# Cross attention of a decoder block: value rows (ctx times Wv Wo) first, then P times them, on one core

## The chip, the cores and the metric

One Trainium2 chip, one of its cores. The metric is device time in microseconds of one execution. Engines are named PE (TensorE, matrix products), ACT (ScalarE), DVE (VectorE), POOL (GpSimd) and SP (SyncE, which issues DMAs).

## What is computed

A decoder block on x (16 batches x 64 tokens x 256), all in float32: a chunked test-time-training attention, then cross attention to ctx (16 x 64 x 128) with 16 heads of width 128, then a gated FFN of 704 with quantised weights and activations. Each of the three is followed by adding its input and a layer norm. The change touches the cross attention alone:

```
q = rmsnorm(x @ Wq); k = rmsnorm(ctx @ Wk); v = ctx @ Wv      # 16 heads of 128
P = softmax(q k^T / sqrt(128))                                # 64 x 64 for each batch and head
out = concat_h(P_h v_h) @ Wo                                  # 2048 -> 256
```

For each head, `v_h` and its 128 rows of Wo come to `ctx (Wv_h Wo_h)`. Both kernels form `mvo`, the product Wv_h Wo_h (128 x 256 for each head, 4096 columns in all), once before the tiles.

## The kernel before

The first half (until about 179 us) is the test-time-training attention over 4 chunks, with key projections for the cross attention placed between its steps. It works in 32x32 blocks (L554, L562, L572): four blocks lie at the partitions 32j..32j+31, for the operands and the output alike, and write one PSUM bank.

The second half is a software pipeline over 8 tiles of 128 tokens (2 batches). `pipeline()` counts i from -2 to 10. In cycle i, PE works in an order that is written out by hand at L738 to L781: the q projection of tile i (`q_quarter`, four quarters of 512 columns, each two products, L626), the transposes of q (L640), the scores of tile i (`scores`, 64 columns for each head and batch, L658), the cross attention's rest for tile i-1, the FFN's gate and up for tile i-2 (`gate_up`, L699) and its down projection for tile i-3 (L717). The output projection of the first half (`ttt_out`, L723) and the transposes of the new x1 (L731) serve tiles i+2 and i+1. ACT and DVE have written-out orders of their own.

The rest of the cross attention for a tile is:

- softmax: DVE (L1379 to L1382, L1393), POOL (L1525, L1527) and ACT (L1011) make P of the scores, and signal `p_ready`;
- `p_transpose` (L649): 8 transposes of 128x128; ACT copies them out as `pt`;
- `context_sum` (L672): 4 products of 64 rows x 512 columns, P times ctx. n=0 and n=1 take the row halves 0..63 and 64..127 of `pt` and `ctx2` one after the other, n=2 and n=3 are placed apart. ACT copies each out as `cxp` (L1006);
- `attention_out` (L680): for each of 16 heads, one product 128x128 by 256 columns, `cxp` times `mvo`, all summed in one bank; eight heads before `x1_transpose` and eight behind it. DVE adds it to x1 (L1402).

PSUM banks: 0 and 1 hold q quarters, 2 and 3 the transposes, 4 and 5 the scores. Banks 6 and 7 are handed out in turns from a list, `turns`; a turn waits on PE until the turn two before it has been copied out (`open_turn`, L608). The list of before holds `down`, four `cp`, `wo`, four `gu` and `y` for each cycle.

The clock column (PEclk, 1.00 or 0.50) is the share of TensorE's 2.4 GHz that was granted. A float32 product of before stands in the trace as two records.

Of the kernel before, what the change touches and what calls it, by code (L numbers as in the profile page):

```python
# [58 lines left out]
def decoder_block(nc, x, ctx_in, Wq, Wk, Wv, Wo, Wbeta, ln_w, ln_b, Wg1, Wg2, norm_w,  # L59
                  XWq, XWk, XWv, XWo, gq, gk, w1_in, w2_in, out):  # L60
    stack = ExitStack()
    with stack:
# [65 lines left out]
        krow1 = place("krow1", BANK, over="ctxt")  # L128
# [63 lines left out]
        qjunk = place("qjunk", BANK)  # L192
        assert cursor[0] <= at_of["xwk"]
        cxp = place("cxp", XH * P)
        gs = place("gs", FF)
        assert cursor[0] <= at_of["pR"]
# [8 lines left out]
        sg = place("sg", FF)  # L205
# [86 lines left out]
        for i, cur, prev, last2, last3, nxt, nxt2 in pipeline():  # L292
            turns += [("down", i - 3, 0, "dve")] * last3
            turns += [("cp", i - 1, n, "act") for n in range(2)] * prev
            turns += [("wo", i + 2, 0, "dve")] * nxt2
            turns += [("cp", i - 1, n, "act") for n in range(2, 4)] * prev
            turns += [("gu", i - 2, n, "dve") for n in range(4)] * last2
            turns += [("y", i - 1, 0, "dve")] * prev
# [23 lines left out]
        def _(sp):  # L322
# [71 lines left out]
            for half in range(2):  # L394
                load(ctx2[half * T:(half + 1) * T, :].rearrange("p (b c) -> p b c", c=CD), ctx_in.rearrange("b s c -> s b c"), "ctx")
# [15 lines left out]
        def _(pe):  # L411
# [251 lines left out]
            def context_sum(i, n):  # L663
                b2, odd = n // 2, n % 2
                if n == 0:
                    pe.wait_ge(sem("tp_evac"), tp_of[("pt", i, 1)] + 1)
                    if i == 0:
                        pe.wait_ge(sem("ld_ctx"), 64)
                bk = open_turn("cp", i, n)
                rows = slice(odd * T, odd * T + T)  # L670
                b = 2 * i + b2
# [886 lines left out]
```

## Time and profile before

| | |
|---|---|
| median of 3 runs | 442.09 us (441.3 to 442.74) |
| the profiled execution | 441.95 us, span of its trace 440.1 us |
| busy: PE, DVE, ACT, POOL | 362.4, 266.0, 218.0, 120.9 us |
| mean granted TensorE clock | 0.919 |
| pipeline over the tiles | from about 179 us to the end |

PE's busy time is a union of overlapping records; how long a group really occupies PE is read from the start of the next group. A timeline row gives the start in the span, its length, the instructions, and in brackets the idle time of the engine before it with what ended it.

### The profile page before, as it was taken

How to read it: one execution, taken by the hardware profiler on the slowest of the kernel's cores; microseconds unless marked ns; L12 is line 12 of the kernel's file. 1: busy time of each engine (PE TensorE's matmuls, PEld its weight loads, DVE VectorE, ACT ScalarE, POOL GpSimd, SP SyncE). 2: the span in 40 equal slices, each digit the busy share in tenths (PEclk: the TensorE clock that was granted, in tenths of full speed). 3: DMA queues.
4: the chain of work that ended last, by engine and by line, in shares of the span. 5: the costliest groups of instructions: out<-in, count | busy, mean ns of one | idle time of the engine just before them, and what ended most of it. 6: DMA issues, size and time to landing. Idle time of an engine off the chain costs nothing.

```text
span 440.1 us, 10666 instructions
## 1 busy us (share of the span) xinstructions
PE 362.4 (82%) x4506; PEld 212.4 (48%) x4506; DVE 266.0 (60%) x494; ACT 218.0 (50%) x584; POOL 120.9 (27%) x132
## 2 busy tenths in 40 slices
PE   3999979779977735596799999999999999996942
PEld 2445844435433212343465665755757557473621
DVE  1579945499996886504243384673946728367564
ACT  3035954545533333063646757468475584753320
POOL 3042891022040041103033332343223432233001
PEclk9999969988968969589899999999999999998975
DMA  8990000000323001901010010100100100000000
GB/s 260 240 365 11 1 4 5 3 4 3 81 75 101 2 0 35 211 7 48 0 41 11 1 48 12 44 6 13 49 12 25 25 14 0 12 3 0 12 0 25
DMA packets 17630, 19.93 MB, mean 45 GB/s; under 512 B 3360, under 2 KB 15024, under 8 KB 17328
## 3 DMA queue, kind: packets, MB, share of 16 engines
q1 hardware_dynamic: 17552, 19.24, 16.0%
q8 instruction: 36, 0.59, 0.6%
q14 instruction: 10, 0.08, 0.1%
q10 hardware_dynamic: 32, 0.02, 0.0%
HBM read 18.07 MB, written 1.18 MB: 44 GB/s over the span
## 4 chain that ended last, share of the span: by engine, by line
PE 50%; DVE 19%; ACT 13%; POOL 8%; issue 7%; DMA 1%; SPq 1%; POOLq 0%; DVEq 0%; ACTq 0%
PE ps L626 9%; PE ps L535 7%; PE ps L672 5%; PE ps L446 5%; PE ps L525 4%; PE ps L680 3%; PE ps L640 3%; PE ps L572 3%; POOL pr L1525 3%; POOL pr L1527 3%; PE ps L554 3%; PE ps L649 2%; DVE pr L1382 2%; DVE pr L1379 2%; DVE mx L1381 2%
## 5 line engine op out<-in xcount | busy, mean ns | idle before, releaser
L626 PE MATMUL ps<-xwq,x1t 128*128 128x512 f32 x128 | 65.0, 638 | 0.9 <-ACT x1t L997 0.9
L680 PE MATMUL ps<-mvo,cxp 128*128 128x256 f32 x256 | 58.4, 382 | 0.1
L680 PEld LDWEIGHTS ps<-mvo,cxp 128*128 128x128 f32 x256 | 47.6, 190 | 6.7 <-issue 0.4
L535 PE MATMUL ps<-ctxt,xwk 128*128 128x512 f32 x64 | 39.0, 716 | 2.4 <-issue 2.2
L975 ACT ACTIVATE qjunk<-ps 128x128 f32<-128x128 f32 x128 | 33.5, 280 | 9.9 <-PE ps L626 9.7
L896 ACT ACTIVATE ksq<-ps 128x512 f32<-128x512 f32 x32 | 19.0, 594 | 38.3 <-PE ps L525 28.2
L626 PEld LDWEIGHTS ps<-xwq,x1t 128*128 128x128 f32 x128 | 24.0, 202 | 27.5 <-issue 24.7
L985 ACT ACTIVATE qt<-ps 128x512 f32<-128x512 f32 x32 | 19.2, 601 | 23.4 <-PE ps L640 23.3
L525 PE MATMUL ps<-ksq,onehot 128*32 128x512 f32 x64 | 21.8, 680 | 9.2 <-ACT ksq L896 9.1
L672 PE MATMUL ps<-pt,ctx 64*128 64x512 f32 x64 | 28.0, 657 | 0.2 <-ACT cxp L1006 0.2
L975 ACT ACTIVATION_READ_ACCUMULATOR qjunk<-ps 128x1 f32 x128 | 27.1, 212 | 0.0
L1525 POOL TENSOR_TENSOR pr<-pr,rq 128x1024 f32<-128x1024 f32 x7 | 13.3, 1901 | 49.1 <-DVE pr L1382 49.1
L1355 DVE TENSOR_TENSOR rr<-ps,xn 128x256 f32<-128x256 f32 x8 | 3.4, 424 | 34.6 <-PE ps L723 34.5
L1362 DVE TENSOR_TENSOR gs<-ps,s 128x352 f32<-128x352 f32 x16 | 8.4, 525 | 25.1 <-PE ps L699 25.1
L1519 POOL TENSOR_TENSOR rq<-rq,mhalf 128x16 f32<-128x16 f32 x8 | 23.3, 2909 | 0.7
L640 PEld LDWEIGHTS ps<-ident,qtok 128*128 128x128 f32 x128 | 15.3, 141 | 16.1 <-issue 12.8
L1508 POOL TENSOR_SCALAR rstd<-mv 128x1 f32<-128x1 f32 x24 | 5.3, 219 | 61.5 <-DVE mv L1318 61.5
L900 ACT ACTIVATE kt<-ps,gks 128x512 f32<-128x512 f32 x32 | 21.8, 682 | 0.0
L1006 ACT ACTIVATE cxp<-ps 128x512 f32<-128x512 f32 x32 | 18.9, 627 | 5.1 <-PE ps L672 5.1
L640 PE MATMUL ps<-ident,qtok 128*128 128x128 f32 x128 | 19.7, 277 | 0.9 <-ACT qtok L976 0.9
L997 ACT ACTIVATE x1t<-ps 128x256 f32<-128x256 f32 x8 | 3.1, 383 | 34.7 <-PE ps L731 34.7
L1323 DVE TENSOR_SCALAR x<-rr,mv,rstd 128x256 f32<-128x256 f32 x16 | 6.6, 413 | 22.5 <-POOL rstd L1509 22.5
(212 smaller groups left out, 736.5 us busy)
## 6 DMA issues: line engine op xcount, KB each, us to landing
rkb<-kscale SPq DMA_DIRECT2D x16, 256.0 KB, 4.0
xn<-in_x_dram SPq DMA_DIRECT2D x4, 512.0 KB, 5.4
ctx<-in_ctx_dram SPq DMA_DIRECT2D x4, 512.0 KB, 8.7
xwo<-in_L_xattn_Wo_dram SPq DMA_DIRECT2D x1, 2048.0 KB, 14.2
xwq<-in_L_xattn_Wq_dram SPq DMA_DIRECT2D x4, 512.0 KB, 5.4
w1n<-in_L_ffn_w_gate_up_dram SPq DMA_DIRECT2D x1, 1408.0 KB, 8.9
xwv<-in_L_xattn_Wv_dram SPq DMA_DIRECT2D x1, 1024.0 KB, 11.0
xwk<-in_L_xattn_Wk_dram SPq DMA_DIRECT2D x1, 1024.0 KB, 16.5
```

What stands on the lines that cost most here:

```text
L446: last = mm(bank(bk), w[:, k * D + hh * P:k * D + (hh + 1) * P], xt[:, k * B * T + half * BANK:k * B * T + (half + 1) * BANK], start=k == ...
L525: mm(bank(5)[rows, :], onehot[:, at:at + 32], ksq[:, (n % 2) * BANK:(n % 2 + 1) * BANK], start=h < 2, stop=h >= XH - 2).then_inc(sem("k_su ...
L535: mm(bank(6 + n % 2), xwk[:, h * XD:(h + 1) * XD], ctxt[:, half * BANK:(half + 1) * BANK], start=True, stop=True)\
L626: last = mm(bank(n % 2), x1t[:, (i % 2) * D + k * P:(i % 2) * D + (k + 1) * P], xwq[qn][:, k * BANK:(k + 1) * BANK], start=k == 0, stop=k ...
L640: last = nc.tensor.transpose(bank(bk, P, t * P), qtok[:, (n % 2) * BANK + t * P:(n % 2) * BANK + (t + 1) * P], ident[:, :])
L672: turn_done(mm(bank(bk), ctx2[rows, b * CD:(b + 1) * CD], pt[rows, :].rearrange("p (h q) -> p h q", q=P)[:, :, b2 * T:(b2 + 1) * T], start ...
L680: last = mm(bank(6 + turn_of[("y", i, 0)] % 2, D), cxp[:, h * P:(h + 1) * P], mvo[:, h * D:(h + 1) * D], start=h == 0, stop=h == XH - 1)
L900: A(o, bank(6 + n % 2).rearrange("p (i t) -> p i t", t=P), ACT.Copy, scale=gks[:, 1:2]).then_inc(sem("key_emptied"), 1)
L975: A(qjunk[:, t * P:(t + 1) * P], bank(n % 2, P, t * P), ACT.Square, accum_out=qraw_ss[:, h:h + 1])
L985: ins = A(qt[:, n * BANK:(n + 1) * BANK], src, ACT.Copy)
L1519: GP.tensor_tensor(rq[:, :], rq[:, :], mhalf[:, :], ALU.pow).then_inc(sem("rq_ready"), 1)
L1525: GP.tensor_tensor(groups(z, T), groups(z, T), spread(rq[:, :], XH, T), ALU.mult).then_inc(sem("z_ready"), 1)
```

## The change

- `context_sum`, `cxp` and the second load of ctx go away. In their place `value_rows` (n = 0 to 7) multiplies the tile's 128 rows of ctx (two batches) with 512 columns of `mvo` each: 8 products of 128x128 by 512 for a tile, which give the value rows of 16 heads. They lie in `vrows` (z0, z1).
- Of these 8 banks ACT copies out 0 to 4, DVE 5 to 7 (for tile 0, ACT all eight).
- `attention_out` multiplies P transposed (64x64 for each batch and head) with the value rows (64 x 256): 32 products for a tile instead of 16, where the two batches of a head use the partitions 0..63 and 64..127, for operands and output alike.
- `p_transpose` does 32 products of a 64x64 block with a piece of the identity instead of 8 transposes of 128x128.
- The value rows of tiles 1 to 7 are spread over the cycle i = tile + 1; those of tile 0 over the cycles i = -1 (four) and i = 0 (four). All take turns in banks 6 and 7.
- The silu of the gate is written over `gs`; `krow1` moves to `qjunk`, for which ACT waits once, before its first use of `qjunk`, until SP has written those rows out.

```diff
@@ PE
-            def context_sum(i, n):
...
-                turn_done(mm(bank(bk), ctx2[rows, b * CD:(b + 1) * CD],
-                             pt[rows, :].rearrange("p (h q) -> p h q", q=P)[:, :, b2 * T:(b2 + 1) * T], start=True, stop=True))
+            def value_rows(i, n):
+                bk = open_turn("z", i, n)
+                turn_done(mm(bank(bk), ctxt[:, i * P:(i + 1) * P], mvo[:, n * BANK:(n + 1) * BANK], start=True, stop=True))
 
             def attention_out(i, heads):
                 for h in heads:
                     if h == 0:
-                        wait(turn_emptied("cp", i, 3))
+                        pe.wait_ge(sem("tp_evac"), tp_of[("pt", i, 1)] + 1)
+                        wait(turn_emptied("z", i, 3))
                         open_turn("y", i)
-                    last = mm(bank(6 + turn_of[("y", i, 0)] % 2, D), cxp[:, h * P:(h + 1) * P], mvo[:, h * D:(h + 1) * D],
-                              start=h == 0, stop=h == XH - 1)
+                    if h == XH // 2:
+                        wait(turn_emptied("z", i, 7))
+                    at = (6 + turn_of[("y", i, 0)] % 2) * BANK
+                    for b2 in range(2):
+                        part = slice(b2 * T, (b2 + 1) * T)
+                        zh = vrows[h // 8][part, (h % 8) * D:(h % 8 + 1) * D]
+                        last = mm(ps[part, at:at + D], pt[part, h * T:(h + 1) * T], zh, start=h == 0, stop=h == XH - 1)
...
@@ PE, p_transpose
-                    for t in range(4):
-                        col = (i % 2) * XH * T + (n * 4 + t) * P
-                        last = nc.tensor.transpose(bank(bk, P, t * P), pr[:, col:col + P], ident[:, :])
+                    for t in range(8):
+                        for b2 in range(2):
+                            part = slice(b2 * T, (b2 + 1) * T)
+                            col = (i % 2) * XH * T + (n * 8 + t) * T
+                            last = mm(ps[part, bk * BANK + t * T:bk * BANK + (t + 1) * T], pr[part, col:col + T], ident[part, part],
+                                      start=True, stop=True)
...
@@ ACT
-            def context_out(i, n):
...
+            def value_rows_out(i, n):
+                bk = turn("z", i, n)
                 if n == 0 and i >= 1:
                     act.wait_ge(sem("turn_done"), turn_of[("y", i - 1, 0)] + 1)
-                o = cxp[:, :].rearrange("p (h r q) -> p r h q", r=2, q=P)[:, odd, :, b2 * T:(b2 + 1) * T]
-                freed(A(o, bank(bk).rearrange("p (h q) -> p h q", q=T), ACT.Copy))
+                freed(A(vrows[n // 4][:, (n % 4) * BANK:(n % 4 + 1) * BANK], bank(bk), ACT.Copy))
...
@@ DVE
+            def value_rows_out(i, n):
+                bk = turn("z", i, n)
+                V.tensor_copy(vrows[n // 4][:, (n % 4) * BANK:(n % 4 + 1) * BANK], bank(bk)).then_inc(sem("turn_dve"), 1)
```

What moves on PE, first place: from the start of a tile's q projection to the transposes of P of the tile before (L626 q quarter, L709 transposes of the FFN's h, L649 transposes of P, L717 down projection). Before:

```order
L626 MATMUL ps<-xwq_154,x1t 128x512 x2
L709 MATMUL ps<-ident_b,hq 128x128 x5
L709 MATMUL ps<-ident_b,hq 64x128
L626 MATMUL ps<-xwq_155,x1t 128x512 x2
L649 MATMUL ps<-ident,pr 128x128 x8
L717 MATMUL ps<-w2t,hqt 128x256 x6
```

After (L639, L723, L664 and L731 are the same functions; L681 is `value_rows`):

```order
L639 MATMUL ps<-xwq_154,x1t 128x512 x2
L681 MATMUL ps<-mvo,ctxt 128x512
L723 MATMUL ps<-ident_b,hq 128x128 x5
L723 MATMUL ps<-ident_b,hq 64x128
L639 MATMUL ps<-xwq_155,x1t 128x512 x2
L681 MATMUL ps<-mvo,ctxt 128x512
L664 MATMUL ps<-ident,pr 64x64 x32
L731 MATMUL ps<-w2t,hqt 128x256 x6
```

Two value products now stand ahead of the transposes of P, which are 32 small products.

Second place on PE: from `ttt_out` to the first half of `attention_out` (L723 `ttt_out`, L640 a transpose of q, L690 that of x for the FFN, L699 gate and up, L658 scores, L680 `attention_out`). Before:

```order
L723 MATMUL ps<-wo,ogt 128x256 x2
L672 MATMUL ps<-pt,ctx_58 128x512
L640 MATMUL ps<-ident,qtok 128x128 x4
L690 MATMUL ps<-ident_b,xq 128x128 x2
L672 MATMUL ps<-pt,ctx_58 128x512
L699 MATMUL ps<-w1t,xqt 128x352 x4
L640 MATMUL ps<-ident,qtok 128x128 x4
L699 MATMUL ps<-w1t,xqt 128x352 x4
L658 MATMUL ps<-kt,qt 64x64 x32
L680 MATMUL ps<-mvo,cxp 128x256 x8
```

After (L737, L653, L704, L713, L674 and L695 are the same functions, L681 is `value_rows`):

```order
L737 MATMUL ps<-wo,ogt 128x256 x2
L681 MATMUL ps<-mvo,ctxt 128x512
L653 MATMUL ps<-ident,qtok 128x128 x4
L704 MATMUL ps<-ident_b,xq 128x128 x2
L681 MATMUL ps<-mvo,ctxt 128x512
L713 MATMUL ps<-w1t,xqt 128x352 x4
L681 MATMUL ps<-mvo,ctxt 128x512
L653 MATMUL ps<-ident,qtok 128x128 x4
L713 MATMUL ps<-w1t,xqt 128x352 x4
L681 MATMUL ps<-mvo,ctxt 128x512
L674 MATMUL ps<-kt,qt 64x64 x32
L695 MATMUL ps<-z_152,pt 64x256 x16
```

Two context sums went, four value products came, two of them between and behind the gate and up products and ahead of the scores.

On DVE, the same place: from the addition behind `ttt_out` to the norm that makes the new x1 (L1355 the addition, L1362 and L1364 gate and up, L1368 silu times up, L1323 the norm; the first softmax step, L1379, follows). Before:

```order
L1355 TENSOR_TENSOR rr<-ps,xn 128x256
L1317 BN_STATS st_135<-rr 128x6
L1318 BN_AGGR mv<-st_135 128x2
L1362 TENSOR_TENSOR gs<-ps,s_62 128x352
L1364 TENSOR_TENSOR us<-ps,s_62 128x352
L1362 TENSOR_TENSOR gs<-ps,s_62 128x352
L1364 TENSOR_TENSOR us<-ps,s_62 128x352
L1368 SCALAR_TENSOR_TENSOR us<-us,sx,sg 128x704
L1323 TENSOR_SCALAR xn<-rr,mv,rstd 128x256
```

After (L1366 is the copy of a value bank, L1422 and L1424, L1430 and L1377 the others):

```order
L1409 TENSOR_TENSOR rr<-ps,xn 128x256
L1371 BN_STATS st_134<-rr 128x6
L1372 BN_AGGR mv<-st_134 128x2
L1366 COPY z_153<-ps 128x512
L1422 TENSOR_TENSOR gs<-ps,s_62 128x352
L1424 TENSOR_TENSOR us<-ps,s_62 128x352
L1366 COPY z_153<-ps 128x512
L1422 TENSOR_TENSOR gs<-ps,s_62 128x352
L1424 TENSOR_TENSOR us<-ps,s_62 128x352
L1366 COPY z_153<-ps 128x512
L1430 SCALAR_TENSOR_TENSOR us<-us,sx,gs 128x704
L1377 TENSOR_SCALAR xn<-rr,mv,rstd 128x256
```

Three copies came in between, one ahead of the gate's, one behind the first pair and one behind the second.

## Rows read from the trace of the kernel before

**Rows 1.** The page's first part, busy time of each engine.

```profile
PE 362.4 (82%) x4506; PEld 212.4 (48%) x4506; DVE 266.0 (60%) x494; ACT 218.0 (50%) x584; POOL 120.9 (27%) x132
```

**Rows 2.** Busy time of each engine in four stretches (window length first; PEclk, DMA last).

```profile
64.65:95.37 30.72, 26.56 (x1048) 13.98 (x1048) 18.56 (x48) 14.85 (x25) 2.58 (x2) 1.00 0.02 5
173.88:190.94 17.06, 10.26 (x17) 5.34 (x18) 7.75 (x16) 2.33 (x11) 1.57 (x4) 0.50 0.79 158
292.18:320.06 27.88, 26.74 (x173) 16.93 (x173) 16.92 (x33) 17.69 (x58) 9.21 (x11) 1.00 0.08 25
402.57:405.98 3.41, 3.41 (x14) 2.14 (x13) 2.91 (x9) 1.19 (x2) 0.17 (x1) 0.50 0.00 0
```

**Rows 3.** Timeline of PE, from P's transposes of tile 3 to those of tile 4.

```profile
292.18 1.09 PE L649 MATMUL ps<-ident,pr 128*128 128x128 f32 x8 [0.82 <-POOL pr L1527]
...
296.31 1.13 PE L672 MATMUL ps<-pt,ctx 64*128 64x512 f32 x4
297.37 1.98 PE L626 MATMUL ps<-xwq,x1t 128*128 128x512 f32 x4
...
304.15 0.47 PE L699 MATMUL ps<-w1t,xqt 128*128 128x352 bf16 x2 [0.28 <-ACT cxp L1006]
...
305.75 2.08 PE L658 MATMUL ps<-kt,qt 128*64 128x64 f32 x64
307.76 3.72 PE L680 MATMUL ps<-mvo,cxp 128*128 128x256 f32 x16
...
311.54 3.62 PE L680 MATMUL ps<-mvo,cxp 128*128 128x256 f32 x16
314.99 1.88 PE L626 MATMUL ps<-xwq,x1t 128*128 128x512 f32 x4
316.71 0.62 PE L709 MATMUL ps<-ident_b,hq 128*128 128x128 bf16 x6
...
320.06 1.09 PE L649 MATMUL ps<-ident,pr 128*128 128x128 f32 x8 [0.82 <-POOL pr L1527]
```

**Rows 4.** Timeline of PE, one set of 32x32 products in the first half.

```profile
76.49 1.56 PE L572 MATMUL ps<-ak,ub 32*32 32x48 f32 x128
77.98 0.70 PE L535 MATMUL ps<-ctxt,xwk 128*128 128x512 f32 x1
```

**Rows 5.** The chain that ended last, in order of time (start, us, what).

```profile
300.66 1.05 PE ps L672 x2
...
305.10 0.60 ACT qt L985
...
309.61 1.24 DVE pr L1379
...
318.10 1.91 POOL pr L1527
```

**Rows 6.** Groups by line: copies out of PSUM (count | busy, mean ns | idle).

```profile
L1362 DVE TENSOR_TENSOR gs<-ps,s 128x352 f32<-128x352 f32 x16 | 8.4, 525 | 25.1 <-PE ps L699 25.1
...
L1006 ACT ACTIVATE cxp<-ps 128x512 f32<-128x512 f32 x32 | 18.9, 627 | 5.1 <-PE ps L672 5.1
```

**Rows 7.** Timeline of PE, first tiles of the pipeline.

```profile
178.80 3.78 PE L723 MATMUL ps<-wo,ogt 128*128 128x256 f32 x8 [8.16 <-DVE ogt L1257]
...
185.16 8.28 PE L626 MATMUL ps<-xwq,x1t 128*128 128x512 f32 x12 [0.47 <-ACT x1t L997]
...
198.23 0.66 PE L640 MATMUL ps<-ident,qtok 128*128 128x128 f32 x4 [0.90 <-ACT qtok L976]
199.57 2.09 PE L658 MATMUL ps<-kt,qt 128*64 128x64 f32 x64 [0.69 <-ACT qt L985]
...
211.73 1.97 PE L649 MATMUL ps<-ident,pr 128*128 128x128 f32 x8 [5.53 <-DVE pr L1397]
...
237.40 1.05 PE L649 MATMUL ps<-ident,pr 128*128 128x128 f32 x8
```

**Rows 8.** Timeline of PE, last tile.

```profile
398.29 0.63 PE L709 MATMUL ps<-ident_b,hq 128*128 128x128 bf16 x6 [1.01 <-DVE hq L1330]
401.95 1.42 PE L649 MATMUL ps<-ident,pr 128*128 128x128 f32 x8 [3.04 <-POOL pr L1527]
...
411.72 7.15 PE L680 MATMUL ps<-mvo,cxp 128*128 128x256 f32 x32
```

More of the change, by code:

```diff
@@ L192, in decoder_block @@
         qjunk = place("qjunk", BANK)
+        krow1 = place("krow1", BANK, over="qjunk")
         assert cursor[0] <= at_of["xwk"]
-        cxp = place("cxp", XH * P)
-        gs = place("gs", FF)
-        assert cursor[0] <= at_of["pR"]
+        vrows = [place("z0", XH * D // 2, over="ctx2"), place("z1", XH * D // 2, over="xwk")]
         xwq = []
@@ L292, in decoder_block @@
         for i, cur, prev, last2, last3, nxt, nxt2 in pipeline():
+            later = i - 1 if i >= 2 and prev else None
+            first = 0 if i == 0 else None
+            if later is not None:
+                turns += [("z", later, 0, "act"), ("z", later, 1, "act")]
             turns += [("down", i - 3, 0, "dve")] * last3
-            turns += [("cp", i - 1, n, "act") for n in range(2)] * prev
+            if first is not None:
+                turns += [("z", 0, 4, "act"), ("z", 0, 5, "act")]
+            if later is not None:
+                turns += [("z", later, 2, "act"), ("z", later, 3, "act")]
             turns += [("wo", i + 2, 0, "dve")] * nxt2
-            turns += [("cp", i - 1, n, "act") for n in range(2, 4)] * prev
-            turns += [("gu", i - 2, n, "dve") for n in range(4)] * last2
+            if i == -1:
+                turns += [("z", 0, n, "act") for n in range(4)]
+            if first is not None:
+                turns += [("z", 0, 6, "act"), ("z", 0, 7, "act")]
+            if later is not None:
+                turns += [("z", later, 4, "act"), ("z", later, 5, "dve")]
+            turns += [("gu", i - 2, n, "dve") for n in range(2)] * last2
+            if later is not None:
+                turns += [("z", later, 6, "dve")]
+            turns += [("gu", i - 2, n, "dve") for n in range(2, 4)] * last2
+            if later is not None:
+                turns += [("z", later, 7, "dve")]
             turns += [("y", i - 1, 0, "dve")] * prev
@@ L738, in _ @@
             for i, cur, prev, last2, last3, nxt, nxt2 in pipeline():
+                later = i >= 2 and prev
                 if cur:
                     q_quarter(i, 0)
+                if later:
+                    value_rows(i - 1, 0)
                 if last3:
@@ L744, in _ @@
                     q_quarter(i, 1)
+                if later:
+                    value_rows(i - 1, 1)
                 if prev:
@@ L1037, in _ @@
                     q_quarter(i, 3)
-                if prev:
-                    context_out(i - 1, 2)
+                if i == -1:
+                    for n in range(4):
+                        value_rows_out(0, n)
+                if i == 0:
+                    value_rows_out(0, 6)
+                if later:
+                    value_rows_out(i - 1, 4)
                 if cur:
                     tp_out("qt", i, 2)
+                if i == 0:
+                    value_rows_out(0, 7)
                 if last2:
                     tp_out("xqt", i - 2)
-                if prev:
-                    context_out(i - 1, 3)
                 if cur:
@@ L1356, in _ @@
                     norm_stats(rr[:, :])
+                later = i >= 2 and prev
+                if later:
+                    value_rows_out(i - 1, 5)
+                if later and not last2:
+                    value_rows_out(i - 1, 6)
+                    value_rows_out(i - 1, 7)
                 if last2:
```

69 lines of the change are left out of this document (43 added, 26 removed).

## The prediction

> **What bounds the kernel now.** I read four views: the busy times, a table of stretches, the timeline of PE over one cycle of the pipeline, and the chain of waits. PE is busy 362.4 of 440.1 us, DVE and ACT far less [rows 1]. In a whole cycle of the pipeline, 27.88 us from the transposes of P of one tile to those of the next, PE is busy 26.74 at clock 1.00, DVE 16.9, ACT 17.7, POOL 9.2 [rows 2]. Its idle time is 0.82 us ahead of the transposes of P and 0.28 ahead of a gate product, 1.10 together [rows 3]. The chain that ended last runs, in that cycle, from a copy of q (305.10) through DVE (309.61) and POOL (318.10) back to PE at 320.06 [rows 5]. So the two nearly balance: PE's work decides, and the softmax of the tile sticks out by 0.8 us. What is added on PE costs its full time, less at most these 1.10 us a cycle.
>
> **Prices on PE.** They are differences of start times. Four records of 512 columns take 316.71 - 314.99 = 1.72 us [rows 3]; a product is two records, so 0.86. Sixteen records of 256 columns take 3.45 (311.54 to 314.99) [rows 3], 0.43 for a product.
>
> *Removed, a cycle:* the first two context sums 1.06 (296.31 to 297.37) [rows 3], the other two 1.05 each [rows 5]. What follows them pays to start again: the q quarter behind lasts 1.98 against 1.88 without such a neighbour [rows 3]; I allow 0.2 for three places. Together 3.36.
>
> *Value rows:* 8 x 0.86 = 6.88. Stationary and moving shapes are those of the q quarters. Nothing in the row says that they could share a pass.
>
> *Transposes of P:* 8 records, 1.09 before [rows 3]. The nearest row to 32 small products with 64 columns is the scores, 64 such records in 2.08 [rows 3]. They run in pairs side by side: at the rate above (0.43 / 512 a column and record) 64 columns are 0.054, and 64 records in sequence would take 3.4. A pair of products takes 0.13. +1.0.
>
> *`attention_out`:* 16 pairs by 256 columns in place of 16 products. The two context sums n=0 and n=1 are a pair already, on row halves: 2 x 512 columns in 1.06 [rows 3], where one alone takes 1.05 [rows 5]. So a pair costs what a product costs. The change of block shape costs some 0.1 each time it occurs (the first q quarter above), and there are three more such changes around the x1 transposes: +0.3.
>
> PE's work in a cycle grows by 6.88 + 1.0 + 0.3 - 3.36 = 4.8 us.
>
> The Trainium skill (TensorEngine Tiling (Array Packing), "Gotcha 1: PSUM Pressure") says that different row tiles cannot access one PSUM bank simultaneously. Here both blocks of a pair write the same bank; by that rule the pairs would run in sequence. The trace speaks against it (rival A, whose time is worked out there).
>
> **What of it shows.** The 1.10 us of idle time are filled: behind the last q transpose PE now has three value products more (one ahead of the scores, two in the next tile's q projection), 2.6 us, plus 0.3, against the wait of 0.82. The chain from the copy of q is 320.06 - 305.10 = 14.96 and keeps its length. The DVE copy of the last value bank lies ahead of L1368 and is hidden by the wait for the silus; the later scores (+0.86) are hidden too: they ended at 307.76, DVE took them at 309.61 [rows 3, 5].
>
> New waits come from banks 6 and 7, which now have 15 turns a cycle instead of 11. A bank is copied out in 0.63 (ACT) [rows 6]; for DVE a copy of 512 columns is not shown, 352 columns take 0.525 [rows 6]; by width 0.53 to 0.76, I take 0.65. A turn of 0.86 beside it hides this. Not hidden: a gate piece lasts less than 0.47 [rows 3], so the value product behind each pair waits for its bank, some 0.2 twice; and ACT takes the value banks 2 and 3 ahead of the transposes of q and the fourth q quarter, so that the bank 4 and the copy of xq come later than today, where PE already waits 0.28. Below: nothing (DVE and ACT are each idle for over 10 us of the cycle [rows 2]). Above: 1.0. I take 0.5. A cycle: 4.8 - 1.1 + 0.5 = +4.2. Its bounds are 3.5 and 5.0.
>
> **The sum.**
> - Full cycles, from the transposes of P of tile 1 to those of tile 6: five x 4.2 = +21.0.
> - Tile 0's first four value rows stand between `ttt_out` and the x1 transposes. The two `ttt_out` end at 182.6 at clock 0.50, which lasts until 190.94 [rows 2, 7]. At that clock four products are 6.9 us; PE has 2.6 us before its q quarters start at 185.16 [rows 7]. But what PE does at half clock then is value products and not q quarters, and the full clock may come earlier. From -0.3 (clock back at once) to +2.4: +1.5.
> - Tile 0's other four: 3.44, of which the two waits of 0.90 and 0.69 [rows 7] take 1.6: +1.8. P of tile 0 follows by a chain (5.53 idle) [rows 7], so that this delay passes on.
> - Tile 0's P to tile 1's (25.67 now, 211.73 to 237.40) [rows 7]: no context sums, but without them PE waits for q copies as in tile 0's cycle (1.6 of which 0.7 is there today): -3.36 + 1.0; two value products +1.7, P +1.0, `attention_out` +0.3: +0.7.
> - Tile 6's P to tile 7's: here PE waits 1.01 and 3.04 [rows 8], and only what stands ahead of the last q transpose counts: P +1.0, five value products +4.3, waits +0.3, context sums -3.36: +2.2.
> - Tile 7's P to its `attention_out` (401.95 to 411.72) [rows 8]: P +1.0, six value products +5.2, context sums -3.36, and PE is less idle ahead of it, so that the 3.41 us at clock 0.50 [rows 2], worth 1.7, may go: between +1.1 and +3.5, I take +1.8. `attention_out` +0.3.
>
> The tail behind it, DVE and ACT work mostly, is unchanged. ACT's new wait for `krow1` costs nothing: the rows are ready before PE starts `ttt_out` at 178.80 (it waits for them), and ACT needs `qjunk` only behind the first q quarter, which starts at 185.16 [rows 7]. The second load of ctx was waited for by nobody on the chain. In all 21.0 + 1.5 + 1.8 + 0.7 + 2.2 + 2.1 = 29.3 us. The profiled execution took 441.95 us (the median is 442.09, so nothing is to be shifted): 471.3, rounded 471.
>
> **Rivals.**
> - *A: the pairs run in sequence.* For: two row halves and one bank. Against: the 32x32 blocks of L572 lie on four row places and write one bank, and 128 records of 48 columns take 77.98 - 76.49 = 1.49 us [rows 4]; in sequence, at the column price above (0.43 / 512), they would take 5.2. Time: `attention_out` +6.9, P +2.0, so 8.9 a cycle over six cycles, 53; tile 0's P 2, tile 6 to 7 some 5, the end 8.9: 540. Chance 0.05.
> - *B: the granted clock falls while PE works in 64x64 blocks for 7 us.* Against: 30.7 us with 32x32 blocks in large part and PE busy 26.56 show 1.00 [rows 2]. At 1.2 GHz `attention_out` and P cost 9 us more a cycle, much as A: 530 to 550. Chance 0.03.
> - *C: the turns bind.* Each value product between others waits 0.2 to 0.3 for a copy, 2 us more a cycle: +10 to +14, 478 to 486. For: two banks and 15 turns in a cycle. Against: ACT and DVE free for a third of it. Chance 0.13.
> - *D: less is paid.* The small blocks cost nothing beyond the pairs' rate, no new wait, and the half-clock stretches at the start and the end go: 3.5 a cycle and +1 to +4 outside, 460 to 464. Chance 0.10.
> - *E: not slower.* A 64x64 pair streams 256 columns in half the time of a full product, 0.22 for 0.43, P's blocks likewise. Then a cycle saves 3.45 + 1.0 against the 4.2, which is -0.25, and the whole comes to 29.3 - 4.45 x 7 = -1.9: 440. It decides from a pair price of 0.22 down. Against: the scores' pairs cost 0.13 for 64 columns, no less than a full product's 0.11. Chance 0.03.
>
> The forecast, 464 to 478, has the remaining 0.66. It is the bounds above summed: cycles 17.5 to 25, start 0.5 to 5, the first cycle 0 to 1.5, the end 3 to 6 would reach from 463 to 479.5. The range of 461 to 483 adds part of D and most of C, 0.66 + 0.05 + 0.09 = 0.8. Faster or slower by 0.3% (1.3 us) is what can be told from no change: faster 0.01, same 0.02, slower 0.97.
>
> **What would show it.** In the timeline of PE: value products 0.86 from start to start behind a q quarter; `attention_out`'s halves about 3.5 each; P's 64 records about 2.1; no wait of PE for POOL ahead of P in the full cycles; P's transposes 32 us apart; waits of PE for DVE's L1366 and ACT's value copies of some 0.5 a cycle. I am wrong if the halves take 7 us (A, or at clock 0.50 B) or under 2 (E), if cycles are 34 us with PE idle (C), or if the distance is 31.4 or less (D).

## The result, and the profile after

The changed kernel took 484.39 us (median of 4 runs, 477.29 to 486.24) against 442.41 for the kernel before in the same session: ratio 1.086 (95% interval 1.070 to 1.102). Two of its four runs, the profiled one among them, are over 1.5% slower than its fastest, and so is one of before; without these, as the ratio is taken, it is 480.1 (477.29 and 482.99) against 442.0. It is slower, as forecast. The size is 38 us and not 29, within the stated 461 to 483 and above the 464 to 478 of the sum. The profiled execution took 486.24 us, 44.3 more than that of before.

The same windows query as in [rows 2] of the changed kernel, for a full cycle, for the cycle from tile 5's P to tile 6's (it has no `ttt_out`), and for the stretch from tile 7's P to its last product:

```profile
283.23:316.12 32.89, 32.27 (x270) 18.12 (x269) 19.14 (x37) 18.17 (x58) 9.21 (x10) 1.00 0.08 21
381.89:414.78 32.89, 31.24 (x266) 17.45 (x265) 17.88 (x33) 18.18 (x58) 8.45 (x8) 1.00 0.02 5
444.70:463.30 18.60, 17.65 (x157) 9.39 (x157) 10.89 (x24) 5.80 (x10) 1.50 (x4) 1.00 0.03 8
```

PE's busy time in a full cycle went from 26.74 [rows 2] to 32.27, its idle time from 1.1 to 0.6. Most of the cycle is still PE's. In the second window PE is idle for 1.65 us although its work is a `ttt_out` less: something else has taken over there (below).

The timeline of PE in the full cycle:

```profile
283.23 2.08 PE L664 MATMUL ps<-ident,pr 64*64 64x64 f32 x64
285.25 0.93 PE L731 MATMUL ps<-w2t,hqt 128*128 128x256 bf16 x6
...
288.37 1.02 PE L681 MATMUL ps<-mvo,ctxt 128*128 128x512 f32 x2
289.23 1.88 PE L639 MATMUL ps<-xwq,x1t 128*128 128x512 f32 x4
290.94 1.02 PE L681 MATMUL ps<-mvo,ctxt 128*128 128x512 f32 x2
...
294.51 1.08 PE L681 MATMUL ps<-mvo,ctxt 128*128 128x512 f32 x2
295.91 0.93 PE L713 MATMUL ps<-w1t,xqt 128*128 128x352 bf16 x4 [0.32 <-ACT xqt L1027]
297.00 1.12 PE L681 MATMUL ps<-mvo,ctxt 128*128 128x512 f32 x2 [0.15 <-DVE gs L1422]
297.96 0.60 PE L653 MATMUL ps<-ident,qtok 128*128 128x128 f32 x4
...
299.48 1.12 PE L681 MATMUL ps<-mvo,ctxt 128*128 128x512 f32 x2
300.54 2.08 PE L674 MATMUL ps<-kt,qt 128*64 128x64 f32 x64
302.55 3.67 PE L695 MATMUL ps<-z,pt 64*64 64x256 f32 x32
306.15 0.44 PE L745 MATMUL ps<-ident,xn 128*128 128x128 f32 x2
306.52 3.67 PE L695 MATMUL ps<-z,pt 64*64 64x256 f32 x32
310.12 1.98 PE L639 MATMUL ps<-xwq,x1t 128*128 128x512 f32 x4
311.94 1.02 PE L681 MATMUL ps<-mvo,ctxt 128*128 128x512 f32 x2
312.80 0.61 PE L723 MATMUL ps<-ident_b,hq 128*128 128x128 bf16 x6
...
315.17 1.02 PE L681 MATMUL ps<-mvo,ctxt 128*128 128x512 f32 x2
316.12 0.39 PE L664 MATMUL ps<-ident,pr 64*64 64x64 f32 x6
```

Read from start to start: P's 64 records take 2.02; the halves of `attention_out` (L695) 3.60 each; a value product (L681) 0.86 behind a q transpose and ahead of a q quarter (288.37 to 289.23), but 0.96 between two gate groups (297.00 to 297.96), 1.06 ahead of the scores (299.48 to 300.54) and 0.95 ahead of P (315.17 to 316.12). No row ahead of P has a wait: the 0.82 us for POOL [rows 3] are gone, as the prediction said. PE's waits come to 0.32 + 0.15.

The chain that ended last does not stay on PE. In this cycle (start, us, what) it runs over ACT for 3.9 us ahead of the gate product:

```profile
292.00 0.48 ACT z L1042
292.50 0.59 ACT qt L1023
293.09 1.03 ACT qjunk L1013 x8
294.12 0.49 ACT qtok L1014
294.61 0.49 ACT z L1042
295.10 0.49 ACT qt L1023
295.58 0.28 ACT xqt L1027
```

Where the time went, by PE's starts: `ttt_out` at 178.80 before and 189.30 after, P of tile 0 at 211.73 and 224.27, of tile 1 at 237.40 and 251.21, of tile 6 at 374.95 and 414.78, of tile 7 at 401.95 and 444.72, the last product of `attention_out` at 418.49 and 462.99.

| stretch | before | after | difference | predicted |
|---|---|---|---|---|
| start to `ttt_out` (same work) | 178.8 | 189.3 | +10.5 | 0 |
| `ttt_out` to P of tile 0 | 32.9 | 35.0 | +2.0 | +3.3 |
| to P of tile 1 | 25.7 | 26.9 | +1.3 | +0.7 |
| five cycles to P of tile 6 | 137.5 | 163.6 | +26.0 | +21.0 |
| to P of tile 7 | 27.0 | 29.9 | +2.9 | +2.2 |
| to the last product of `attention_out` | 16.5 | 18.3 | +1.7 | +2.1 |
| the tail | 21.6 | 21.4 | -0.2 | 0 |

So 34.0 us lie where 29.3 were predicted, and 10.5 where the two programs do the same work. In the five cycles it is +5.1 and three times +5.0 where there is a `ttt_out`, and +5.9 (27.01 to 32.89) where there is none.

### The profile page after: what moved, and what is told of

It reads as the page before. It is cut to its first block, busy times and chain, and to the rows that moved or that the text cites. A ratio compares the mean times of both kernels' runs of the same rounds, so it can differ in the third digit from the quotient of the medians.

```text
span 484.4 us, 12225 instructions
## 1 busy us (share of the span) xinstructions
PE 407.9 (84%) x5274; PEld 224.1 (46%) x5274; DVE 280.4 (58%) x515; ACT 224.2 (46%) x595; POOL 121.0 (25%) x132
## 4 chain that ended last, share of the span: by engine, by line
PE 62%; DVE 16%; ACT 11%; issue 5%; POOL 3%; DMA 1%; SPq 1%; POOLq 0%; DVEq 0%; ACTq 0%
PE ps L639 11%; PE ps L695 10%; PE ps L681 9%; PE ps L548 6%; PE ps L459 4%; PE ps L664 4%; PE ps L538 3%; PE ps L674 3%; PE ps L585 3%; PE ps L567 2%; ACT qjunk L1013 2%; PE ps L653 2%; DVE gs L1422 2%; PE ps L713 2%; ACT qt L1023 1%
## 5 line engine op out<-in xcount | busy, mean ns | idle before, releaser
L681 PE MATMUL ps<-mvo,ctxt 128*128 128x512 f32 x128 | 67.9, 618 | 2.4 <-DVE gs L1422 1.3
L639 PE MATMUL ps<-xwq,x1t 128*128 128x512 f32 x128 | 62.2, 611 | 1.2 <-ACT x1t L1035 1.2
L695 PE MATMUL ps<-z,pt 64*64 64x256 f32 x512 | 58.3, 379 | 0.0
L695 PEld LDWEIGHTS ps<-z,pt 64*64 64x64 f32 x512 | 34.6, 133 | 19.6 <-issue 1.8
L639 PEld LDWEIGHTS ps<-xwq,x1t 128*128 128x128 f32 x128 | 22.8, 191 | 25.7 <-issue 22.9
L1042 ACT ACTIVATE z<-ps 128x512 f32<-128x512 f32 x43 | 26.6, 619 | 17.3 <-PE ps L681 17.3
L538 PE MATMUL ps<-ksq,onehot 128*32 128x512 f32 x64 | 24.4, 744 | 8.7 <-ACT ksq L932 8.6
L681 PEld LDWEIGHTS ps<-mvo,ctxt 128*128 128x128 f32 x128 | 21.6, 192 | 21.2 <-issue 9.7
L1366 DVE COPY z<-ps 128x512 f32<-128x512 f32 x21 | 14.5, 692 | 26.5 <-PE ps L681 26.5
L653 PEld LDWEIGHTS ps<-ident,qtok 128*128 128x128 f32 x128 | 15.9, 141 | 17.1 <-issue 15.6
L664 PE MATMUL ps<-ident,pr 64*64 64x64 f32 x512 | 18.3, 231 | 5.5 <-DVE pr L1459 4.9
L664 PEld LDWEIGHTS ps<-ident,pr 64*64 64x64 f32 x512 | 17.1, 146 | 11.7 <-DVE pr L1459 5.7
```

Of the source, the lines that this page charges most:

```text
L538: mm(bank(5)[rows, :], onehot[:, at:at + 32], ksq[:, (n % 2) * BANK:(n % 2 + 1) * BANK], start=h < 2, stop=h >= XH - 2).then_inc(sem("k_su ...
L639: last = mm(bank(n % 2), x1t[:, (i % 2) * D + k * P:(i % 2) * D + (k + 1) * P], xwq[qn][:, k * BANK:(k + 1) * BANK], start=k == 0, stop=k ...
L653: last = nc.tensor.transpose(bank(bk, P, t * P), qtok[:, (n % 2) * BANK + t * P:(n % 2) * BANK + (t + 1) * P], ident[:, :])
L664: last = mm(ps[part, bk * BANK + t * T:bk * BANK + (t + 1) * T], pr[part, col:col + T], ident[part, part], start=True, stop=True)
L681: turn_done(mm(bank(bk), ctxt[:, i * P:(i + 1) * P], mvo[:, n * BANK:(n + 1) * BANK], start=True, stop=True))
L695: last = mm(ps[part, at:at + D], pt[part, h * T:(h + 1) * T], zh, start=h == 0, stop=h == XH - 1)
```

## The experiments

### Do the 10 us of the first half belong to the change?

Both kernels again, unchanged.

> The changed kernel once more, for a second profile. In the first one the half ahead of the tiles (where both kernels do the same work) ended 10.5 us later than in the kernel before (PE's ttt_out starts at 189.30 against 178.80), and the tiles took 33.8 us more, of which the full cycles are 32.88 against 27.88. Theory 1: the tiles' part is fixed (cycles 32.9 again, within 0.1), and the 10.5 us of the first half vary from execution to execution: here ttt_out starts anywhere from 178 to 190. Theory 2: they belong to the changed kernel (a longer program, whose instructions PE fetches in blocks): 187 to 191 again.

> The kernel before once more, for a second profile. Both theories: cycles of 27.9. Theory 1: ttt_out starts anywhere from 178 to 190, as for the changed kernel. Theory 2: 177 to 180 again. Time 441 to 453.

The changed kernel took 481.57 us (479.5 to 487.14), 1.081 (1.073 to 1.089) of a before of 445.04; the kernel before, as a run of its own, 448.09 (443.91 to 453.85). Three rows of PE's timeline, the first of the changed kernel as first profiled, then of its second profile and of the second profile of before:

```profile
189.30 3.78 PE L737 MATMUL ps<-wo,ogt 128*128 128x256 f32 x8 [8.16 <-DVE ogt L1307]
```

```profile
183.45 3.38 PE L737 MATMUL ps<-wo,ogt 128*128 128x256 f32 x8 [8.16 <-DVE ogt L1307]
```

```profile
190.07 3.78 PE L723 MATMUL ps<-wo,ogt 128*128 128x256 f32 x8 [8.16 <-DVE ogt L1257]
```

The kernel before reaches `ttt_out` at 178.80 [rows 7] in one execution and at 190.07 in another. The order is turned round. The share of the tiles repeats: from `ttt_out` to the end 261.2 us before (451.3 - 190.07) and 295.4 after (478.9 - 183.45), +34.2, with cycles of 27.88 and 32.88. So the tiles cost 34 us more, and the 10.5 of the first half need no change of the kernel to appear. Whether a few microseconds of them belong to the change all the same is not settled: over the profiles of this study `ttt_out` starts at 182.7 on average in the five of kernels built on the one before (178.8 to 190.1) and at 186.9 in the eight built on the changed one (183.1 to 190.0), and the spread within each, 11.3 and 6.9, is larger than that difference. The interval of the ratio 1.081, 1.073 to 1.089, is 32.6 to 39.5 us: the tiles' 34 alone fit into it, and so do 34 and 5 more.

### Do the pairs run side by side?

`att_seq`: all 8 products of one batch, then all 8 of the other, instead of alternating. Same work.

```diff
-                for h in heads:
...
-                    for b2 in range(2):
-                        part = slice(b2 * T, (b2 + 1) * T)
+                for b2 in range(2):
+                    part = slice(b2 * T, (b2 + 1) * T)
+                    for h in heads:
```

> The changed kernel with the 16 products of each half of attention_out in another order: 8 heads of the lower 64x64 blocks, then 8 heads of the upper ones. The result is the same. Theory (blocks at different row and column halves share PE's time when they stand next to one another): a half takes about 7 us in place of 3.6, a cycle 32.9 + 7 = 40, the whole some 45 us more than the changed kernel, about 525. Rival (each block costs a quarter or half of a full product by its size, whatever stands next to it): no change, 484.

517.35 us, 1.161 (1.152 to 1.171). PE's timeline:

```profile
352.21 6.31 PE L695 MATMUL ps<-z,pt 64*64 64x256 f32 x32
358.45 0.44 PE L745 MATMUL ps<-ident,xn 128*128 128x128 f32 x2
```

The same 32 records take 6.24 in sequence and 3.60 alternating; the cycle is 38.16, +5.28 (twice 2.64), somewhat less than expected, because a block alone takes 6.24 / 16 = 0.39 and not 0.43. Rival A is out: alternating, the pairs do run side by side, both into one PSUM bank, and a pair costs 7.20 / 16 = 0.45, about what a full product costs (0.43).

### What do P's small blocks cost?

`p_whole`: the transposes of P as before, 8 of 128x128. `attention_out` then multiplies other elements of `pt` than it should; its shapes and counts are the same.

```diff
-                    for t in range(8):
-                        for b2 in range(2):
-                            part = slice(b2 * T, (b2 + 1) * T)
-                            col = (i % 2) * XH * T + (n * 8 + t) * T
-                            last = mm(ps[part, bk * BANK + t * T:bk * BANK + (t + 1) * T], pr[part, col:col + T], ident[part, part],
+                    for t in range(4):
+                        col = (i % 2) * XH * T + (n * 4 + t) * P
+                        last = nc.tensor.transpose(bank(bk, P, t * P), pr[:, col:col + P], ident[:, :])
```

> The changed kernel, but P is transposed in 8 blocks of 128x128 as before, so that attention_out multiplies other elements of P than it should (the output is wrong; the amount of all later work is the same). Theory (a cycle is PE's work, its cost the 1.0 us of the small blocks): cycles 31.9 in place of 32.9, the whole 7 us less, 474 to 478. Rival (the chain of the softmax has taken over, PE's work is hidden): less than 2 us.

471.38 us, 1.056 (1.047 to 1.066); cycle 31.64, -1.24.

```profile
337.36 1.02 PE L678 MATMUL ps<-mvo,ctxt 128*128 128x512 f32 x2
338.21 1.04 PE L662 MATMUL ps<-ident,pr 128*128 128x128 f32 x8
339.09 0.92 PE L728 MATMUL ps<-w2t,hqt 128*128 128x256 bf16 x6
```

P takes 0.88 instead of 2.02, and the value product ahead of it 0.85 (337.36 to 338.21) instead of 0.95. That second difference is the price of a change of block shape, by a run that changes nothing else there. The Trainium skill (TensorEngine Tiling (Array Packing), "Key Properties") says that changing the tiling mode drains the engine. This place agrees, with about 0.1 us.

### How much of the cycle is the value products'?

`half_values`: value rows 4 to 7 are left out, products, turns and copies; `attention_out` takes the first eight heads' rows for all sixteen.

```diff
+                if n >= 4:
+                    return
...
-                        zh = vrows[h // 8][part, (h % 8) * D:(h % 8 + 1) * D]
+                        zh = vrows[0][part, (h % 8) * D:(h % 8 + 1) * D]
```

> The changed kernel with only value rows 0 to 3 of each tile: the products and copies of 4 to 7 are left out, and heads 8 to 15 are multiplied with the rows of heads 0 to 7 (the output is wrong; P, attention_out and all else keep their amount). Theory (a cycle is PE's work): in the trace of the changed kernel the places of these four take 0.86, 1.40 (with a wait of 0.33 for ACT), 0.96 and 1.06 us, 4.3 together; cycles of 28.6 in place of 32.9, each with PE waiting less than 1 us, the whole some 28 us less, 450 to 456. Rival (the softmax or the copies bind by now): cycles of 30 or more.

462.86 us, 1.034 (1.024 to 1.045); cycle 29.70, -3.2. The windows view of its cycle, and PE's timeline ahead of the gate:

```profile
309.80:339.50 29.70, 28.10 (x261) 16.93 (x260) 16.91 (x33) 17.67 (x57) 9.20 (x10) 1.00 0.09 24
```

```profile
322.04 0.77 PE L715 MATMUL ps<-w1t,xqt 128*128 128x352 bf16 x4 [1.60 <-ACT xqt L1029]
```

PE's busy time falls by 4.17 (32.27 to 28.10), but its idle time grows by 1.0, and the wait for the copy of xq from 0.32 to 1.60. The cycle of 29.70 lies between the theory's 28.6 and the rival's 30. From the start of value product 3 to the gate it is 4.48 us (317.56 to 322.04) for 4.97 (290.94 to 295.91). Two value products of 0.85 and 1.08 are gone from that stretch and it is shorter by 0.49, just the copy of one value bank on ACT (0.48 from start to start). So ahead of the gate it is ACT that decides, in the changed kernel too.

### Are DVE's three copies worth anything?

`act_all`: ACT copies banks 5, 6 and 7 too, between its copies of xq, q and the gate's silus.

```diff
-                turns += [("z", later, 4, "act"), ("z", later, 5, "dve")]
+                turns += [("z", later, 4, "act"), ("z", later, 5, "act")]
...
-                turns += [("z", later, 6, "dve")]
+                turns += [("z", later, 6, "act")]
```

> The changed kernel with all eight value banks copied out by ACT, none by DVE. Theory (P is ready 2.6 us ahead of PE, at 313.51 for a start at 316.12, and ACT and DVE have time left): moving three copies to ACT makes the silus and P later by up to 2 us, which this slack takes; cycles 32.9 within 0.3. Rival (the banks that DVE empties are what keeps the change from costing more): cycles longer by 1 us or more, the whole by 6 or more.

482.73 us, 1.083 (1.072 to 1.094), against 1.081 for the change itself; cycle 32.89, the same. The cycle to tile 7's P is longer, 31.99 for 29.94. In the full cycles it does not matter who empties these banks.

### Is ACT's order what makes PE wait for xq?

`act_order`: ACT takes the last q quarter ahead of value bank 3 and of the copy of the second q transposes.

```diff
                     value_rows_out(i - 1, 2)
+                if later and not cur:
                     value_rows_out(i - 1, 3)
                 if cur:
-                    tp_out("qt", i, 1)
-                    q_quarter(i, 3)
+                    if later:
+                        q_quarter(i, 3)
+                        value_rows_out(i - 1, 3)
+                        tp_out("qt", i, 1)
...
```

> The changed kernel with ACT taking the fourth q quarter out before the value bank 3 and the transposes of q number 1, and not behind them. Theory (in a cycle PE waits 0.32 us at the gate product, 1.19 in the cycles without ttt_out, because ACT's copies of bank 3, q and bank 4 come one after the other behind a value product): these waits go or fall under 0.1 and 0.5; cycles of 32.6, the ones without ttt_out 32.2, the whole 2 to 3 us less. Rival (the wait only moves on to the next turn of banks 6 and 7): cycles as before.

489.09 us, 1.101 (1.093 to 1.108); cycle 34.38, +1.5. The rival had the place, a turn of banks 6 and 7, but not the size: value bank 3 now comes out late, and the value product that takes the turn two behind it waits.

```profile
327.43 1.12 PE L681 MATMUL ps<-mvo,ctxt 128*128 128x512 f32 x2 [1.42 <-ACT z L1042]
```

The quarter's copy itself cannot go earlier, since it overwrites `qtok`, which PE's second q transposes must have read; they stand behind it on PE. So PE's order has to change with ACT's.

`after_qt1` does that. On PE the second q transposes go ahead of the last q quarter, and ACT takes bank 3 behind that quarter.

```diff
                     value_rows(i - 1, 2)
                 if cur:
-                    q_quarter(i, 3)
+                    q_transpose(i, 1)
+                    q_quarter(i, 3)
                 if later:
                     value_rows(i - 1, 3)
-                if cur:
-                    q_transpose(i, 1)
...
@@ ACT
-                    value_rows_out(i - 1, 3)
                 if cur:
                     tp_out("qt", i, 1)
                     q_quarter(i, 3)
+                if later:
+                    value_rows_out(i - 1, 3)
```

> The changed kernel with the transposes of q number 1 ahead of the fourth q quarter on PE, and ACT's copies in the same order (value bank 3 behind the fourth quarter). In the runs so far PE waited at the gate product for ACT's copy of xq, and ACT's copies there began with the fourth quarter, which waits until those transposes have freed their half of qtok. Theory (this chain on ACT is the second limit of a cycle): the wait of 0.32 us goes, and that of 1.19 in the cycle without ttt_out falls under 0.7; cycles 32.5 in place of 32.88, the whole 2 us less. Rival (a wait of the same length at the turn of value bank 4): cycles 32.9 or more.

479.61 us, 1.077 (1.069 to 1.085). The cycles with `ttt_out` are 33.44 (+0.55), the two without 32.04 and 29.10 (-0.85 and -0.84). In a cycle with it:

```profile
357.01 1.12 PE L681 MATMUL ps<-mvo,ctxt 128*128 128x512 f32 x2 [0.48 <-ACT z L1041]
...
360.38 0.47 PE L713 MATMUL ps<-w1t,xqt 128*128 128x352 bf16 x2 [0.32 <-DVE z L1366]
```

The wait for xq is gone, and two turn waits have come. In the full cycles the turns of banks 6 and 7 lie close behind (the rival was right there); without `ttt_out` it was ACT, as the theory had it. Together it is no gain: from `ttt_out` to the end 295.4 us (480.7 - 185.34), as without the exchange.

`qt1_before` is the control, the same exchange on PE in the kernel before:

> The kernel before with only that exchange on PE: the transposes of q number 1 ahead of the fourth q quarter. A control for the next kernel. Theory (the cycle of the kernel before is bound by PE up to the gate product and by the softmax behind it; ACT has a little slack there): cycles 27.6 to 27.9. If the order alone is worth 1 us a cycle, the pairs of the next kernel are not what it gains by.

445.75 us, 1.002 (0.998 to 1.006), cycle 27.83. In the full cycles the exchange alone is worth nothing there; the two cycles without `ttt_out` are 26.6 for 27.0 (352.16, 378.74 and 405.31 are the starts of P).

### What is in the kernel before, used well?

The pairs run side by side, and the kernel before has one such pair in sequence: context sums 2 and 3 (row halves) are placed apart. `pair_before` puts them next to each other behind the transposes of xq, and gives one of the copies to DVE. It also moves two groups of q transposes back: number 1 behind `ttt_out`, number 2 behind the pair.

```diff
                     q_quarter(i, 3)
-                    q_transpose(i, 1)
                 if nxt2:
                     ttt_out(i + 2)
-                if prev:
-                    context_sum(i - 1, 2)
-                if cur:
-                    q_transpose(i, 2)
+                if cur:
+                    q_transpose(i, 1)
                 if last2:
                     x_transpose_q(i - 2)
                 if prev:
+                    context_sum(i - 1, 2)
                     context_sum(i - 1, 3)
+                if cur:
+                    q_transpose(i, 2)
...
```

> The kernel before with its context sums 2 and 3 next to each other, as 0 and 1 already are, behind the transposes of x for the FFN and ahead of the transpose of q number 2; bank 3 is copied out by DVE. The output is the same. Theory (two products on different row halves cost the time of one): 1.05 us less in each full cycle, of which a wait of about 0.25 at the gate product is given back; cycles of 27.0 in place of 27.88, the whole 5 to 7 us less than the kernel before. Rival (the softmax binds the cycle of the kernel before, whose PE waits 0.82 us for it): no gain.

448.19 us, 1.002 (0.996 to 1.008), cycle 27.74 of 27.88. No gain:

```profile
274.87 1.23 PE L672 MATMUL ps<-pt,ctx 64*128 64x512 f32 x4
276.03 0.66 PE L640 MATMUL ps<-ident,qtok 128*128 128x128 f32 x4
277.89 0.76 PE L699 MATMUL ps<-w1t,xqt 128*128 128x352 bf16 x4 [1.20 <-ACT cxp L1006]
```

The pair takes 1.16 for two times 1.05, and PE then stands 1.20 ahead of the gate for ACT's copy, 0.92 more than before. What PE saves (0.94) is lost again. But the run does not show that a pair alone is worth nothing. ACT copies q transposes 1 out at 274.87, 3.33 us behind the start of the fourth q quarter (271.54); in the kernel before it is 2.46 (299.83 - 297.37). That delay of 0.87 is the length of `ttt_out`, which now stands ahead of them, and ACT's copies up to the gate follow one another without a gap.

`pair_qt3` takes the pair with another order around it: q transposes 1 ahead of the last quarter (so that ACT copies it sooner), number 2 ahead of the pair, and all q transposes ahead of the gate (so that the scores and the softmax come sooner). On PE it is, from the first context sums on: q transposes 1, q quarter 3, `ttt_out`, q transposes 2, xq, context sums 2 and 3, q transposes 3, gate and up.

```diff
                 if cur:
-                    q_quarter(i, 3)
                     q_transpose(i, 1)
+                    q_quarter(i, 3)
...
-                if prev:
-                    context_sum(i - 1, 2)
...
                 if prev:
+                    context_sum(i - 1, 2)
                     context_sum(i - 1, 3)
-                if last2:
-                    gate_up(i - 2, range(0, 2))
                 if cur:
                     q_transpose(i, 3)
                 if last2:
+                    gate_up(i - 2, range(0, 2))
                     gate_up(i - 2, range(2, 4))
```

> The kernel before with its context sums 2 and 3 next to each other (a pair), and the order around them changed so that ACT isn't late: transposes of q number 1, fourth q quarter, ttt_out, transposes number 2, those of x, the pair, transposes number 3, then the four gate and up pieces. DVE copies bank 3 of the four out. The output is the same. Theory (two row halves cost the time of one, and the copies of ACT are the second limit): from the end of the fourth q quarter to the scores 5.0 to 5.5 us in place of 6.56, the silus and with them P earlier by over 1 us, so that PE no longer waits for P; cycles 25.6 to 26.5 in place of 27.88, the whole 10 to 16 us less than the kernel before. Rival (the four gate and up pieces in a row wait for DVE's copies as long as the pair saves): cycles of 27.5 or more.

435.6 us (430.2 to 439.09) against 444.36: 0.975 (0.967 to 0.982). It is faster than both kernels, with the cross attention of before. Its cycle in the windows view, and in PE's timeline:

```profile
289.48:315.48 26.00, 25.50 (x174) 16.86 (x173) 17.52 (x34) 17.07 (x56) 9.21 (x11) 1.00 0.08 27
```

```profile
298.33 1.23 PE L672 MATMUL ps<-pt,ctx 64*128 64x512 f32 x4
299.49 0.66 PE L640 MATMUL ps<-ident,qtok 128*128 128x128 f32 x4
300.24 0.76 PE L699 MATMUL ps<-w1t,xqt 128*128 128x352 bf16 x4
301.40 0.81 PE L699 MATMUL ps<-w1t,xqt 128*128 128x352 bf16 x4 [0.41 <-DVE gs L1363]
```

The cycle is 26.00 for 27.88 [rows 2]: 1.24 less PE work (26.74 to 25.50, of which the pair, 1.16 for 2.10, is 0.94) and 0.6 less idle time. The waits of 0.82 ahead of P and 0.28 ahead of the gate [rows 3] are gone, one of 0.41 for DVE has come. No run has this order without the pair, so how the gain divides between the pair and the order is open; `qt1_before` only shows that one of the exchanges gives nothing by itself in a full cycle.

## Why the forecast came out as it did

**What bounds.** Right in the main. The full cycles of the changed kernel are 98% PE, at clock 1.00, and P is ready (313.51) 2.6 us before PE comes to it (316.12). Its chain from the last copy of q (298.60) is 14.9 us long, as assumed. What the prediction did not see is the stretch from value product 3 to the gate: 4.97 us with `ttt_out` in it (290.94 to 295.91) and 4.97 without (389.60 to 394.57). There ACT's copies decide in both, and PE waits for them.

**The removed context sums.** Predicted 3.36. The added terms below as shown (7.48, 1.14, 0.34) make 8.96, and the busy time grew by 5.53, so 3.4 were given back; this is a difference and was not measured by itself.

**The eight value products.** This is the term that was mis-sized: "8 x 0.86 = 6.88". The rows give 7.48 without waits: four of the eight take 0.86 or 0.85, the one behind the xq transposes 1.08 (1.40 less the wait of 0.32; in `after_qt1`, where no wait follows it, 1.07), between the gate groups 0.96, ahead of the scores 1.06, ahead of P 0.95. The price was read from q quarters that stand among their like and applied to places next to bf16 products and 64-column blocks. The prediction had that cost in view, but allowed it only for `attention_out`. `p_whole` shows it for one place (0.95 to 0.85); for the places next to bf16 products it is read from rows, and no run varies the neighbour alone. It is not any bf16 neighbour: the value product ahead of the transposes of the FFN's h takes 0.86 (311.94 to 312.80). The three that cost 0.96 to 1.08 directly follow bf16 products.

**P and `attention_out`.** Predicted +1.0 and +0.3. P takes 2.02 where the whole transposes take 0.88 (`p_whole`), +1.14, and from the first half of `attention_out` to the next q quarter it is 302.55 to 310.12, 7.57 for 7.23 [rows 3], +0.34. The step "a pair costs what a product costs" holds, and `att_seq` shows why it had to be asked: in sequence it would have been 6.24 for 3.60. The page named in the prediction (the Trainium skill, TensorEngine Tiling (Array Packing), "Gotcha 1: PSUM Pressure") says that different row tiles cannot access one bank at once. The measurement says they can, here with outputs on different partitions of it, and it decides. One sum of rival A does not come out of its rows: 64 records of P in sequence are 3.4, which is 1.3 more than the scores' 2.08 and not 2.0; its 540 would be some 5 us lower.

**The waits.** Predicted 0.5, and 0.47 are there, but not where the signs had them (DVE's L1366 and ACT's value copies): 0.32 at the gate for ACT's copy of xq, 0.15 at the value product behind it for DVE's copy of the gate. With the 1.1 filled, net -0.6 was predicted and the idle time went from 1.1 to 0.6. A full cycle is therefore +5.0 instead of +4.2: +5.5 of busy time less 0.5, where it was to be +4.8 less 0.6. That is the stated upper bound. By busy time 0.60 of the missing 0.8 are the value products. But 0.22 of these belong to the product at 294.51, in the stretch where ACT decides; a cheaper product there would only have lengthened the wait of 0.32.

**The cycle without `ttt_out`.** It was counted like the others, +4.2, and is +5.9. This step failed. The kernel before has its idle time there as well, in other places:

```profile
347.94:374.95 27.01, 25.96 (x169) 16.24 (x169) 15.38 (x29) 17.11 (x54) 8.44 (x9) 1.00 0.02 6
```

```profile
359.00 0.96 PE L699 MATMUL ps<-w1t,xqt 128*128 128x352 bf16 x4 [0.65 <-ACT xqt L989]
374.95 1.09 PE L649 MATMUL ps<-ident,pr 128*128 128x128 f32 x8 [0.37 <-POOL pr L1527]
```

Of its 1.05 us of idle time only 0.4 are ahead of P. The 0.65 at the gate are a wait for ACT's copy of xq, and ACT's copies were to grow. So the idle time was not filled but rose to 1.65: +5.3 of busy time and +0.6 of idle time, where -0.6 was predicted. ACT's timeline of the changed kernel there:

```profile
390.66 0.60 ACT L1042 ACTIVATE z<-ps 128x512 f32<-128x512 f32 x1 [0.83 <-PE ps L681]
...
394.06 0.45 ACT L1027 ACTIVATE xqt<-ps 128x256 bf16<-128x256 bf16 x1
```

and PE's behind it:

```profile
394.57 0.77 PE L713 MATMUL ps<-w1t,xqt 128*128 128x352 bf16 x4 [1.19 <-ACT xqt L1027]
```

From the copy of value bank 3 (390.66) ACT works without a gap until xq is out, 3.9 us (the lines left out are the same work as in the chain of the full cycle above). With `ttt_out` (0.87) in PE's queue PE waits 0.32 for it, without it 1.19: just the missing work. A second wait, at the value product behind the gate, goes from 0.15 to 0.32. `after_qt1`, which changes this order, gets its 0.85 back in the two cycles without `ttt_out` and in none of the others.

**The ends.** `ttt_out` to P of tile 0 +2.0 for +3.3, to tile 1 +1.3 for +0.7, to tile 7 +2.9 for +2.2, the last stretch +1.7 for +2.1: each within 1.3 us, and together +8.0 for +8.3. The stretch at clock 0.50 behind the last P [rows 2] is gone (the third window above shows 1.00), so that PE's added work there was partly paid by the clock, as the +1.8 assumed.

**What the sum could not contain.** The forecast was made against an execution whose first half took 178.8 us. In the twelve other profiles of this study that point lies between 180.4 and 190.1. Of the 38 us (480.1 less 442.0) the tiles make 34.0, 4.7 more than their terms; the other 4 lie ahead of them. The second profile of the changed kernel shows the same: 478.9 less 440.1 is 38.8, of which 4.65 are the first half (183.45 less 178.80). That 480.1 is inside the stated range is luck in part. The tiles alone would have given 476, inside the 464 to 478 of the sum; the rest of the range was added for rival C, and 480 lies in C's band (478 to 486) but not by its mechanism: C wanted 2 us of turn waits a cycle, and there are 0.47.

What a value product costs next to a bf16 group by itself was not tried, nor was a change of the blocks' order that would group equal shapes.

## To carry to other kernels

Price an added product at the place where it will stand: ahead of another block shape or behind products of another type it cost 0.1 to 0.2 us more than among its like, and over eight short products in a 28 us cycle this was the largest error (0.60 us) of a full cycle's sum. When PE decides by less than a microsecond, look for the second limit in the leanest cycle and not in the typical one: saved PE time (`half_values`, `pair_before`) and missing PE work (the cycle without `ttt_out`) both went into waits for ACT's copies ahead of the gate. And when blocks that can run side by side are put next to each other, see what the move does to the copies behind them: with q transposes moved behind `ttt_out` it was 1.002, with them moved forward 0.975.

## What the chip did that was not expected

- Blocks of 64x64 on different rows and columns that write one PSUM bank run side by side when they alternate (3.60 us for 32 records of 256 columns) and not when each kind stands in a row (6.24). A block that stands among its own kind takes 0.39 us, a full product 0.43.
- The time to the same point of the same program (`ttt_out`) differed by 11.3 us between two executions, 178.80 and 190.07. Windows of the kernel before up to there, in the first profile and then in the second:

```profile
0.00:178.80 178.80, 136.58 (x3130) 72.12 (x3131) 128.50 (x227) 78.23 (x146) 51.00 (x54) 0.90 0.27 77
```

```profile
0.00:190.07 190.07, 143.83 (x3131) 75.50 (x3131) 128.30 (x227) 78.31 (x146) 51.03 (x54) 0.89 0.27 72
```

  Of the 11.3 us, 7.3 are PE's busy time, with the same instructions. The clock of 0.50 falls on other groups. One that both have, in the first profile and in the second:

```profile
82.52 1.13 PE L535 MATMUL ps<-ctxt,xwk 128*128 128x512 f32 x2 [2.17 <-issue]
```

```profile
86.67 2.08 PE L535 MATMUL ps<-ctxt,xwk 128*128 128x512 f32 x2 [2.17 <-issue]
```

  The granted clock is 1.00 from 82.52 to 86.16 in the first and 0.50 from 86.67 to 92.39 in the second. Waits of PE for nothing that the profile shows ("issue"), up to 3.9 us long, explain at most 1.5 of it: between 50 us and `ttt_out` they come to 14.8 us in the first profile and 16.3 in the second. What these waits are, and why the clock falls at one place in one execution and at another in the next, stays open.
